# Padding the short contraction products of a gated cross-attention kernel to 128 rows

## What is computed

```
x = x + tanh(g_xattn[i]) * attention_i(layernorm(x), ctx)
x = x + tanh(g_ffn[i])   * ffn_i(layernorm(x))            # i = 0..3
```

```
h   = silu(x @ Wg[e]) * (x @ Wu[e])
out = sum over e of  weight[token, e] * (h @ Wd[e])
```

## Time and profile before

| what | value |
|---|---|
| median of 3 runs | 3338.69 us (3334.62 to 3344.5) |
| the profiled execution, first to last instruction | 3365.5 us |
| PE busy in it | 2862.9 us, 85% |
| PEld, DVE, ACT, POOL busy | 1571.2, 1372.8, 1214.8, 955.8 us |
| mean granted TensorE clock | 0.906 of 2.4 GHz |
| attention 0, F1, F2 in its span | about 58 to 486, 1090 to 1353 and 1939 to 2521 us |

### The profile page before, as it was taken

The page is one execution under the profiler, slowest core; times in us unless marked ns, Lnnn a source line. Parts: engine busy times, 40 slices in busy tenths (PEclk is TensorE's granted clock), DMA queues, the critical chain, the costliest instruction groups (busy, mean ns, idle before and its releaser), DMA issues.

```text
span 3365.5 us, 42519 instructions
## 1 busy us (share of the span) xinstructions
PE 2862.9 (85%) x10639; PEld 1571.2 (47%) x10639; DVE 1372.8 (41%) x3284; ACT 1214.8 (36%) x4294; POOL 955.8 (28%) x967
## 2 busy tenths in 40 slices
PE   5999998898997999899999899999997757642553
PEld 3666667444442444466666544444443333212442
DVE  2333333666665333444443232323226646551112
ACT  3444432455453111555555422111115524411120
POOL 3111110333346000333333100000003344446665
PEclk9999999898898999999999899999997867765777
DMA  4000001000002000000000210000002100001665
GB/s 150 1 1 0 0 1 34 1 1 1 0 1 93 0 0 0 1 1 1 2 1 1 60 49 26 1 1 0 0 0 65 61 1 7 7 6 39 138 148 129
DMA packets 91549, 86.91 MB, mean 26 GB/s; under 512 B 22067, under 2 KB 85059, under 8 KB 90580
## 3 DMA queue, kind: packets, MB, share of 16 engines
q1 hardware_dynamic: 73524, 62.49, 6.4%
q0 software_dynamic: 17824, 22.20, 3.4%
HBM read 66.80 MB, written 17.89 MB: 25 GB/s over the span
## 4 chain that ended last, share of the span: by engine, by line
PE 65%; DVE 10%; issue 10%; ACT 5%; POOL 4%; DMA 4%; another core or an unknown queue 1%; DVEq 1%; SPq 0%; POOLq 0%; ACTq 0%
PE ps L131 59%; DMA moe_sum<-work,weights 3%; PE ps L841 2%; ACT work L906 2%; POOL slots L2082 1%; PE ps L501 1%; DVE n_mx L931 1%; PE ps L220 1%; ACT work L594 1%; PE ps L209 1%; POOL rk L390 1%; DVE ksq L378 1%; POOL moe_sum L2183 1%; PE ps L361 1%
## 5 line engine op out<-in xcount | busy, mean ns | idle before, releaser
L131 PE MATMUL ps<-work,weights 128*128 128x512 f32 (+3 forms) x2540 | 1102.7, 559 | 21.7 <-ACT work L2216 7.9
L131 PE MATMUL ps<-xn_T,weights 128*128 (+3 forms) x2096 | 901.7, 572 | 21.8 <-DMA weights<-in_L_ffn_Wd 7.3
L131 PEld LDWEIGHTS ps<-work,weights 128*128 128x128 f32 (+2 forms) x2540 | 422.7, 196 | 450.6 <-issue 406.4
L131 PEld LDWEIGHTS ps<-xn_T,weights 128*128 128x128 f32 (+1 forms) x2096 | 383.2, 193 | 367.2 <-issue 340.0
L906 ACT ACTIVATE work<-ps,n_negm 128x128 f32<-128x128 f32 (+2 forms) x1024 | 333.2, 349 | 296.4 <-DVE n_rinv L940 168.6
L988 POOL TENSOR_TENSOR work<-work,n_rinv 128x512 f32<-128x512 f32 (+2 forms) x256 | 215.5, 854 | 342.0 <-DVE n_rinv L940 341.9
L251 POOL TENSOR_TENSOR rstd<-var,neg_half 128x4 f32<-128x4 f32 x32 | 32.4, 1013 | 881.4 <-DVE var L237 881.4
L1420 ACT ACTIVATE work<-ps 128x512 f32<-128x512 f32 (+1 forms) x144 | 86.0, 597 | 517.6 <-PE ps L131 517.5
L131 PEld LDWEIGHTS ps<-work 128*128 128x128 f32 (+1 forms) x1624 | 204.3, 186 | 142.1 <-issue 141.8
L131 PE MATMUL ps<-work 128*128 128x128 f32 (+1 forms) x1624 | 243.2, 285 | 0.9 <-ACT work L1337 0.8
L674 POOL TENSOR_TENSOR work<-work,rinv 128x512 f32<-128x512 f32 x128 | 133.1, 1040 | 354.5 <-DVE rinv L627 326.9
(11 more groups left out here) (238 smaller groups left out, 3206.0 us busy)
## 6 DMA issues: line engine op xcount, KB each, us to landing
weights<-in_L_ffn_gate_up_proj SPq DMA_DIRECT2D x16, 768.0 KB
weights<-in_L_ffn_W SPq DMA_DIRECT2D x52, 128.0 KB, 2.3
weights<-in_L_ffn_down_proj SPq DMA_DIRECT2D x16, 384.0 KB
moe_sum<-weights POOLq DMA_DIRECT2D x2, 2176.0 KB
weights<-in_L_xattn_Wo SPq DMA_DIRECT2D x2, 2048.0 KB, 12.6
weights<-in_L_xattn_Wq SPq DMA_DIRECT2D x2, 2048.0 KB, 12.5
weights<-moe_sum SPq DMA_DIRECT2D x8, 512.0 KB, 7.5
xn_rows<-xn SPq DMA_DIRECT2D x5, 512.0 KB, 2.9
```

The lines of the kernel that those rows point to most:

```text
L131: return nc.tensor.matmul(out, lhsT, rhs, start=start, stop=stop, skip_group_check=True)
```

## The change

`ones_b` becomes a 128x128 tile: cleared, then ones in row 0. All 128 partitions of `mask_bias` are cleared before row 0 is written. The mask product then contracts over 128 rows, of which 127 are zero. `const_made` is waited for at 3.

In both mixtures the tile of the split weights gets 128 columns per batch (`c_all`), of which the first 24 or 48 are `c3` as before; the whole is cleared once, in the first body, between `router_sub` and `router_top`. The transposes turn all 128 columns, `ct` and `sel` have 128 partitions, `make_sel` and the copies work on 128 partitions, and the weight product contracts over 128 rows. No product is added or taken away, and the order of the work stays.

```diff
@@ tiles
-    ones_b = sb("ones_b", [1, P], BF16)
+    ones_b = sb("ones_b", [P, P], BF16)
@@ wide_pe
-                    mm(B5, ones_b[0:1, :], mask_bias[0:1, tok(S.of(i))], True, False)
+                    mm(B5, ones_b[:], mask_bias[:, tok(S.of(i))], True, False)
@@ Dense
-            self.c3 = tile(WK, o, TB * self.E3 // 2).bitcast(BF16).rearrange("p (t x e) -> p t x e", t=TB, x=3)
-            o += TB * self.E3 // 2
+            self.c_all = tile(WK, o, TB * P // 2).bitcast(BF16).rearrange("p (t c) -> p t c", t=TB)
+            self.c3 = self.c_all[:, :, 0:self.E3].rearrange("p t (x e) -> p t x e", x=3)
+            self.c_zero = tile(WK, o, TB * P // 2)
+            o += TB * P // 2
@@ weights_turn
-            last = nc.tensor.transpose(b7[0:A.E3, t * P:(t + 1) * P], A.c3[:, t, :, :].rearrange("p x e -> p (x e)"), ident_b[:])
+            last = nc.tensor.transpose(b7[:, t * P:(t + 1) * P], A.c_all[:, t, :], ident_b[:])
@@ weights_out
-        nc.scalar.activation(A.ct[0:A.E3, :], B7.bitcast(BF16)[0:A.E3, 0:W], ACT.Copy).then_inc(A.ct_ready.sem, 1)
+        nc.scalar.activation(A.ct, B7.bitcast(BF16)[:, 0:W], ACT.Copy).then_inc(A.ct_ready.sem, 1)
@@ dense_pe
-                mm(B6, A.sel[0:A.E3, m * P:(m + 1) * P], A.ct[0:A.E3, :]).then_inc(A.w_mm.sem, 1)
+                mm(B6, A.sel[:, m * P:(m + 1) * P], A.ct).then_inc(A.w_mm.sem, 1)
@@ dense_dve, first body
             router_sub(dve, A.r, s, link)
+            nc.vector.memset(A.c_zero, 0.0)
             router_top(dve, A.r, s, link, over_all)
@@ make_sel (its two other lines alike)
-            part = tmp.bitcast(BF16)[0:A.E3, 0:A.cols]
+            part = tmp.bitcast(BF16)[:, 0:A.cols]
@@ prep_act_engine
-        nc.scalar.activation(F2.sel[0:F2.E3, :], l2_sel_made.bitcast(BF16)[0:F2.E3, :], ACT.Copy).then_inc(sel_moved, 1)
+        nc.scalar.activation(F2.sel, l2_sel_made.bitcast(BF16), ACT.Copy).then_inc(sel_moved, 1)
@@ PE's block
-        pe.wait_ge(const_made, 2)
+        pe.wait_ge(const_made, 3)
@@ DVE's block
-        nc.vector.memset(ones_b[:], 1.0).then_inc(const_made, 1)
+        nc.vector.memset(mask_bias, 0.0)
+        nc.vector.memset(ones_b[:], 0.0).then_inc(const_made, 1)
+        dve.wait_ge(const_made, 2)
+        nc.vector.memset(ones_b[0:1, :], 1.0).then_inc(const_made, 1)
```

More of the change, by code:

```diff
@@ L1492, in make_sel @@
             if x == 0:
-                ordered(nc.gpsimd.tensor_copy(sel[0:A.E3, :], part))
+                ordered(nc.gpsimd.tensor_copy(sel, part))
             else:
-                ordered(nc.gpsimd.tensor_tensor(out=sel[0:A.E3, :], in0=sel[0:A.E3, :], in1=part, op=ALU.add))
+                ordered(nc.gpsimd.tensor_tensor(out=sel, in0=sel, in1=part, op=ALU.add))
     L1E, L1F, L1K = 8, 176, 2
```

## The result

The kernel after takes 3284.5 us (median of 4 runs, 3280.2 to 3290.1), the one before 3338.3 on the same chip (4 runs). The ratio is 0.983 with an interval of 0.981 to 0.985: faster, by 49 to 65 us. The forecast was 3281.

What follows compares the result with a forecast made beforehand. The prediction took PE's own sequence to bound attention 0, F1 and F2. Savings of 39.8 us in the mixtures and 18.9 in attention 0, less 0.8 added, took 3338.7 us to 3281 us, ratio 0.983; range 3268 to 3320.

Steps and rivals of the forecast that it cites:

- The bound: In attention 0, F1 and F2 PE is busy throughout, so each microsecond off PE's own sequence shortens the run.
- Attention 0: Padding the mask product removes 0.295 us in each of 64 heads, 18.9 us in all.
- The hidden bf16 matmul: A bf16 matmul of 512 columns with its load hidden costs 0.215 us, half of a float32 one.
- Type counts for nothing on the way in: In the mixtures, a bf16 load of 128 rows behind a float32 one costs 0 of the 0.20 us ahead.
- rival A: Bf16 loads aren't drawn ahead of float32 matmuls, so only the way out is gained, 19 us: 3320 us; chance 0.12.
- The mixtures: Padding the weight products of F1 and F2 and the transposes of their weights saves 39.8 us.
- 0.30 for every product: In the mixtures, 126 weight products each lose a hole of 0.30 us, 37.8 us in all.
- The products ahead of the router's: In the mixtures, four weight products before the narrow router's product gain only 0.20 us each, 0.8 us in all.
- F1's weights: Widened weight transposes in the mixtures: six groups within PE's sequence gain 0.20 us each, 1.2 us in all.
- What was added: `make_sel` on 128 partitions costs 0, the `mask_bias` memset 0.5 us and the `c_zero` memsets 0.3 us: 0.8 us.
- From span to median: Whole kernel: the 57.9 us saving is taken from the median, 3338.7 us, which is 26.8 us below the profiled span.
- rival D: Attention 1 and the last stages run at changing clocks and may move both ways by some us; no separate chance.

Runs made afterwards that it cites:

- second trace of after: The changed kernel run once more, unaltered, on another chip beside other variants: 3310.3 us, ratio 0.983 to the kernel before.
- no_mask: The changed kernel without the mask product; the scores start their own accumulation and the mask is left out: 3296.5 us.
- mask_only: The kernel before with only attention 0's mask product padded to 128 rows, mixtures left at 24 and 48 rows: 3351.2 us, ratio 0.995.
- rows64: The changed kernel with its mask and weight products contracting over only 64 of the 128 prepared rows: 3365.5 us, ratio 0.999 to the kernel before.
- f32_mask: The kernel before with its one-row mask product in float32 instead of bf16: 3406.1 us in one run, beside 3369.4 for the kernel before.
- mix_only: The changed kernel with the mask's lines as before, so only the two mixtures are padded: 3324.0 us, ratio 0.986 to the kernel before.
- rows65: The changed kernel with its mask and weight products contracting over only 65 of the 128 prepared rows: 3308.0 us, ratio 0.982 to the kernel before.

## Why the prediction was right, step by step

**The bound** held. In the three stages PE stayed busy but for 0.63 us, so what was saved on it came off the time: 18.2 us came off attention 0, and 10.6 and 27.3 off F1 and F2, in the second trace of after (its stages end at 555.7, and take 254.4, 466.8 and 137.2 us). The sum is 56.1; predicted were 57.9.

**Attention 0**: predicted 64 x 0.295 = 18.9. The stretch of a head lost 0.29, and 64 of these are 18.6. The start took none of it back.

**The hidden bf16 matmul**, of which no row told the price, was taken as 0.215 from a bound of 0.23; no_mask has 0.20 to 0.22.

**Type counts for nothing on the way in.** This was the step without a row, and rival A its failure: 0.76 ahead of the load, 5.57 for a chunk. The trace has 0.24 and 5.37.

**The mixtures** were predicted at 39.8 and gave 37.9. The size of the step was right only where the next operation is a product of 512 columns. From all loads of the bf16 product, each interval between two of them within a mixture, before against the second trace of after:

| what follows the product | intervals | before | after | gain |
|---|---|---|---|---|
| product over 128 rows | 65 | 5.67 | 5.37 | 0.30 |
| transposes over 128 rows | 47 | 6.06, 6.28 or 6.71 | 5.81, 6.02 or 6.46 | 0.25 |
| router's product, 8 or 16 columns (bodies 2 and 3) | 4 | 7.48 | 7.38 | 0.10 |
| transposes of 8 rows (F1, chunk 1) | 3 | 5.86 | 5.90 | -0.04 |
| transposes of 16 rows (F2, chunk 1) | 3 | 6.02 | 5.91 | 0.11 |

These are 122 of the 130 intervals; the other 8 hold the transposes of the weights or a first body's wait. The terms that were mis-sized:

- I took 0.30 for every product. Behind 47 of them stand transposes, and there it is 0.25: 2.4 us too much.
- The products ahead of the router's were given 0.20 and have 0.10: 0.4 us. Behind the narrow product the router's load started 0.32 us later, as a wide one does; behind the padded one it is 0.73, so a way in to 8 or 16 columns is now to be paid.
- F1's weights are transposed directly behind a product, and the two were given 0.50 together. Behind 24 rows the way in to 24 columns was already paid, and the interval went from 5.99 to 5.64: 0.45 us too much over three bodies. In F2, where they don't touch, it is 0.50 to 0.56.
- In chunk 1 the product is followed by the transposes of the router's result, 8 rows in F1 and 16 in F2. This I had not seen: I asked which neighbour stays narrow and found only the router's product. 1.0 us in F1 and 0.6 in F2.

That is 4.8 us, and 39.8 less 4.8 is 35.0. All intervals but the two in which a first body waits give 34.7. So the agreement of 37.9 with 39.8 is in part luck: of the remaining 3 us, 1.4 are in the first bodies' intervals (9.10 to 8.63 in F1 and 9.54 to 8.63 in F2) and the rest lies ahead of the first load and behind the last, and the first bodies vary without the change. In the other traces F2's is anything from 6.98 to 9.15, and mask_only, which leaves F2 as it was, has the stage before the last body at 485.3 us where before has 487.6.

The last of the four is the most instructive. The weight loads there in F1, in before and then in the second trace of after:

```profile
1164.36 0.19 PEld L131 LDWEIGHTS ps<-work,weights 128*128 128x128 f32 x1 [0.24 <-issue]
1165.30 0.09 PEld L131 LDWEIGHTS ps<-work,weights 24*128 24x128 bf16 x1 [0.76 <-issue]
1165.32 0.48 PEld L1244 LDWEIGHTS ps<-ident,work 8*128 8x128 f32 x4
1165.82 0.30 PEld L131 LDWEIGHTS ps<-xn_T,weights 128*128 128x128 f32 x2
```

```profile
1135.40 0.19 PEld L131 LDWEIGHTS ps<-work,weights 128*128 128x128 f32 x1 [0.24 <-issue]
1135.83 0.10 PEld L131 LDWEIGHTS ps<-work,weights 128*128 128x128 bf16 x1 [0.24 <-issue]
1136.56 0.32 PEld L1244 LDWEIGHTS ps<-ident,work 8*128 8x128 f32 x4 [0.64 <-issue]
1136.90 0.30 PEld L131 LDWEIGHTS ps<-xn_T,weights 128*128 128x128 f32 x2
```

Before, the 24-row product and the 8-row transposes stand one behind the other without a hole between them: one way in and one way out for both. After, the product is wide and the transposes alone are narrow; the way in has moved behind the product, 0.64 us of idle ahead of the load. From the last down load to the next float32 load it takes 1136.90 - 1135.40 = 1.50 us, where it was 1.46. So the padding is worth nothing there, and it is the largest single reason why F1 gave 10.6 us instead of 13.

That two narrow ones have no hole between them isn't general, though. In F2 the 48-row product stands ahead of 16-row transposes, and in rows64 64 rows stand ahead of F1's same 8-row transposes. Both have the 0.23 us of idle time that a narrow product has ahead of a wide one:

```profile
1948.46 0.09 PEld L131 LDWEIGHTS ps<-work 48*128 48x128 bf16 x1 [0.76 <-issue]
1948.78 0.32 PEld L1244 LDWEIGHTS ps<-ident,work 16*128 16x128 f32 x4 [0.23 <-issue]
```

```profile
1164.89 0.09 PEld L131 LDWEIGHTS ps<-work,weights 64*128 64x128 bf16 x1 [0.76 <-issue]
1165.21 0.32 PEld L1244 LDWEIGHTS ps<-ident,work 8*128 8x128 f32 x4 [0.23 <-issue]
```

So 48 and 64 rows differ from 8 and 16 as they do from 128, and 24 rows don't differ from 8. Where between 24 and 48 rows that second step lies no run shows. It accounts for the table's -0.04 us in F1 and 0.11 in F2: that interval of F1 is 5.86 us over 24 rows in before and 6.01 over 64 in rows64, the same 0.15 apart.

**What was added** was taken as 0.8 us and can't be seen. POOL's timeline at the start has its two-input operation of 1408 columns at 2.83 us on 24 partitions in before (first line) and at 2.84 on 128 in after, 2.0 ns a column as in the earlier trace rows:

```profile
24.73 2.83 POOL L1495 TENSOR_TENSOR weights<-weights 24x1408 bf16<-24x1408 bf16 x1
24.79 2.84 POOL L1498 TENSOR_TENSOR weights<-weights 128x1408 bf16<-128x1408 bf16 x1
```

DVE's memset of the mask's tile took 0.91 us (it writes 32-bit words, so half of the 1.8 that I had as the upper bound), and the second memset 0.11.

```profile
10.93 0.91 DVE L2519 MEMSET weights<- 128x1024 uint32 x1 [0.58 <-DVE y_T L2513]
```

The first mask load starts at 59.4 us instead of 59.7.

**From span to median.** The sum was set against the median, 26.8 us below the profiled span, and not against the span; that was right: what the change saves doesn't depend on it, and the median is the metric. What lies behind F2 takes 839 to 843 us in every other trace of this study, before's included, and 817.8 in after's first. The 26.8 us by which before's span is longer than its median have that size. That before's other runs had the short last part is inferred from this, since they left no trace. The length goes with the chip as far as is known: after's first trace is the only one known to be from the first chip, and the eight of the two other chips are all long. Before's span of 3365.5 us is 21 above the longest of its runs on the first chip and within those on the others (3352.5 to 3381.5); on which chip that trace was taken isn't known. Attention 1 takes 489 to 498 us: 498.2 in before and 497.6 in rows64, 492.2 in f32_mask, 490.1 in mask_only, 489.0 in mix_only, though none of them touches it. That was rival D's region. It doesn't follow the holes, since f32_mask has all of them; what decides it is open.

The Trainium skill ("TensorE: Matmul & The Clock Gate", the table under "Why this matters for your kernels") says that one matmul over K = 32 takes the time of one over K = 128. For the matmul by itself the trace agrees (389 ns over 24 or 48 rows, 379 and 384 over 128). For its place between full products it doesn't: 0.51 us for the mask product over one row and some 0.21 padded, and rows64 against rows65 shows it for one row more. The Trainium skill's page "TensorEngine Tiling (Array Packing)", under "Key Properties", states that a change of tiling mode drains the engine, and the modes that it lists under "Available Configurations" have 128, 64 or 32 rows. The page doesn't say in which mode a plain product over few rows runs, so that the holes are such changes is a reading, not shown. The traces fit it: up to 64 rows there is a hole on entering and leaving, from 65 there is none; between 24 and 8 rows there is none, and between 48 or 64 rows and 16 or 8 there is one.

## What to carry to other kernels

Look for products over 64 rows or fewer (or 48 columns and fewer, the widest that were compared) between full ones in PE's stretches, by the idle time ahead of their loads and of the loads behind them: here, between float32 products of 512 columns at 2.4 GHz, a way in of 0.20 and a way out of 0.10 us each, saved with zero rows where both neighbours are wide. Ahead of the load it isn't always 0.76: behind short transposes the 32-row load shows 0.17 and only the wide load after it 0.76. Price each by its own neighbours, since next to another narrow product the hole may only move. To gather narrow ones together instead was not tried; by the traces it should help where they are alike (24 rows ahead of 8) and not where they aren't (48 or 64 rows ahead of 16 or 8). Then ask who waits next: where PE was alone on the path 56 of 58 us came, in attention 1 20 of 48.

## What the runs showed of the hardware that was not expected

- The step lies between 64 and 65 rows: 3365.5 us against 3308.0, idle time ahead of the load 0.76 against 0.24.
- A narrow load doesn't have a hole by itself. An 8-row float32 load starts 0.02 us after a 24-row bf16 load (1165.30, 1165.32); the hole belongs to a change: between wide and narrow, and between 48 or 64 rows and 16 or 8 (0.23 us of idle time).
- A float32 product over one row has a hole of 0.39 us, a bf16 one 0.295.
- The last part of the kernel has two lengths, 817.8 us and 839 to 843, and the long one came with before, after and every variant. The short one was seen once, on the first chip; whether the chip decides it wasn't tried.
- Few columns count as few rows do. The transposes of F2's weights, 48 columns wide in before and 128 in the second trace of after (first and second line), had the same 0.76 us ahead of their load and lost it:

```profile
2091.29 0.23 PEld L1332 LDWEIGHTS ps<-ident_b,work 128*48 128x48 bf16 x4 [0.76 <-issue]
```

```profile
2046.02 0.10 PEld L1334 LDWEIGHTS ps<-ident_b,work 128*128 128x128 bf16 x1 [0.24 <-issue]
```
